# State space stage: one scan instruction of 1024 columns a unit in place of two of 512, its decays in two buffers

## The chip, the cores and the metric

The kernel runs on one core of one Trainium2 chip. The metric is the device time in microseconds (us) from launch to end; less is better. The engines that matter here are TensorE (PE), VectorE (DVE), ScalarE (ACT), GpSimd (POOL) and SyncE (SP), which issues the DMAs of this stage. SBUF and PSUM are the two on-chip memories.

## The reference

A pre-norm layer with a state space block (Mamba) is followed by a pre-norm layer with attention and a mixture of eight experts. The input is 16 sequences of 1024 tokens of 256 features, in fp32. The change is in the state space block only, whose heart is this recurrence over the tokens, for 512 channels d and 16 states n:

```python
def step(h, inp):
    d_t, B_t, C_t, u_t = inp
    dA = jnp.exp(d_t[:, :, None] * A)
    h = h * dA + (d_t * u_t)[:, :, None] * B_t[:, None, :]
    y = jnp.einsum('bdn,bn->bd', h, C_t)
    return (h, y)
```

`d_t` (delta) is a softplus of a projection, `u_t` the convolved input, `y + u * D` is gated by `silu(z)` and projected out. The decay `dA` differs for each channel, state and token.

## The kernel before

The program runs four stages one after the other: the state space stage (lines 79 to 768), attention, routing, experts. Only the first changes.

**Tiling.** Each of the 16 sequences is cut into two halves of T = 512 tokens. The 512 channels are four groups of 128 (the partitions). A half is worked as 32 units: two passes of two channel groups each (PC = 2), and in a pass the 16 states. So a unit is one state `n` of two channel groups `c`, 128 x 2 x 512 elements, and there are 16 x 2 x 32 = 1024 units. For the second half of a sequence the scan starts from `h_end`, which holds the last column of every unit of the first half.

**One unit.** SyncE loads the row B of the state on all partitions (`bb`), and the row C (`cb` or `cv`). GpSimd multiplies `du` by `bb` to `dbu` (line 361, 128x1024). ScalarE makes the decays, one `Exp` of 512 columns for each channel group, into `decay` in PSUM (line 512). VectorE scans each group (line 622, `tensor_tensor_scan`, h = h * decay + dbu). The state is then weighed by C to `prod`: by GpSimd in 13 of 32 units (line 370, u % 5 in 1 and 3), by VectorE in the other 19 (line 604), where ScalarE has first copied the row C into PSUM as `c_bank` (line 499). TensorE sums the products of the 16 states in PSUM by matmuls with the identity (line 739).

**Rings.** `bb`, `dbu`, `h` and `prod` are rings of four units (RING). `decay` has one slot for each of the two groups, all of it two PSUM banks; `c_bank` has one, `y_bank` two, and three `side` banks serve the preparation of the next half (normalisation, input projection, convolution, delta, silu), which all engines do between the steps of the units, at the 64 positions of a hand-written table (SIDE).

**Order.** Every engine has its own program, written out by hand; the engines meet only at semaphores. GpSimd's order for unit u is: make `dbu` of unit u + 2, then weigh unit u - 1 if that is its own. The waits around the scan are:

```python
wait(act, scan_done, scans_done(q, u - 1, cc))   # ScalarE, before decay[:, cc] of unit u
wait(pool, scan_done, scans_done(q, u - RING))   # GpSimd, before dbu of unit u
wait(pool, scan_done, scans_done(q, u))          # GpSimd, before it weighs unit u
```

Of the kernel before, what the change touches and what calls it, by code (L numbers as in the profile page):

```python
# [8 lines left out]
ALU = mybir.AluOpType  # L9
# [3 lines left out]
P = 128  # L13
# [5 lines left out]
T = 512  # L19
# [41 lines left out]
def mamba_stage(nc, x, w, x1, rows_bc):  # L61
# [65 lines left out]
    with ExitStack() as ctx:  # L127
# [31 lines left out]
        sp_r = sb("sp_r", [P, CH, T])  # L159
# [42 lines left out]
        decay_done = sem("decay_done")  # L202
        scan_done = sem("scan_done")
# [33 lines left out]
        def scans_done(q, u, cc=PC - 1):  # L237
            return count(q, POSITIONS, PC * u + cc + 1)
# [91 lines left out]
        def _(pool):  # L330
# [24 lines left out]
            def make_dbu(q, u):  # L355
                p, slot = u // NS, u % RING
                wait(pool, b_loaded[slot], count(q, 16 * (UNITS // RING), 16 * (u // RING + 1)))
                wait(pool, scan_done, scans_done(q, u - RING))
                if u % NS == 0:
                    wait(pool, du_done, count(q, PASSES, p + 1))  # L360
                nc.gpsimd.tensor_tensor(  # L361
                    dbu[:, slot], du[:, q[1], p * PC:(p + 1) * PC], bb[:, slot].unsqueeze(1).to_broadcast([P, PC, T]),
                    ALU.mult).then_inc(dbu_done, 1)

            def weigh_state(q, u):
                k, slot = POOL_UNITS.index(u), u % RING
                wait(pool, c_loaded[C_BUFFER[k]], count(q, 16 * loads_into(C_BUFFER, k), 16 * loads_into(C_BUFFER, k, k + 1)))
                wait(pool, scan_done, scans_done(q, u))
# [32 lines left out]
        def _(act):  # L401
# [7 lines left out]
            act.wait_ge(s_a, 4)  # L409
# [12 lines left out]
            def take(q, kind, i):  # L422
# [26 lines left out]
                elif kind == "dbl":  # L449

                    wait(act, rows_stored, count(before(before(q)), 32, 32))
                    ins = nc.scalar.copy(dbl[:, r], bank)
                elif kind == "dt":
                    if i == 0:
                        wait(act, delta_done, count(q, CH, 0))
                    nc.scalar.activation(sp_r[:, i], bank, ACT.Relu, bias=vecs[:, 1, i:i + 1])
                    ins = nc.scalar.activation(bank, bank, ACT.Abs, bias=vecs[:, 1, i:i + 1])
# [34 lines left out]
            def save_end(q, u):  # L492
                wait(act, scan_done, scans_done(q, u))
                nc.scalar.copy(h_end[:, u], h[:, u % RING, :, T - 1]).then_inc(end_saved, 1)

# [5 lines left out]
            def scan_block(q, last, norm):  # L501
                r = q[1]
                wait(act, delta_done, count(q, CH, CH))
                for u in range(UNITS):
                    n = u % NS
                    for cc in range(PC):
                        c = u // NS * PC + cc
                        to, earlier = unit_at(q, u - 2)
                        if cc and earlier in VECTOR_UNITS:
                            copy_c(q, vector_upto(earlier) % VU)  # L510
                        wait(act, scan_done, scans_done(q, u - 1, cc))
                        nc.scalar.activation(decay[:, cc], delta[:, r, c], ACT.Exp,  # L512
                                             scale=a_neg[:, c, n:n + 1]).then_inc(decay_done, 1)
                        if not last:
                            prepare(after(q), PC * u + cc, norm)
# [12 lines left out]
        def _(dve):  # L528
# [56 lines left out]
            def preparation(q, v, norm):  # L585
# [7 lines left out]
                if dt_of and dt_of[0] == "dt":  # L593
                    c = dt_of[1]
                    wait(dve, soft_done, count(p, 2 * CH, 2 * c + 2))
                    nc.vector.tensor_tensor(delta[:, p[1], c], side_bank[:, bank_of("dt", c)], sp_r[:, c],
                                            ALU.add).then_inc(delta_done, 1)

            def weigh_state(q, u):
                slot = u % RING  # L600
                wait(dve, scan_done, scans_done(q, u))
# [5 lines left out]
            def scan_block(q, last, norm):  # L607
                r = q[1]
                for u in range(UNITS):
                    n, slot = u % NS, u % RING  # L610
                    for cc in range(PC):
                        wait(dve, decay_done, scans_done(q, u, cc))
                        if cc == 0:
                            wait(dve, dbu_done, units_done(q, u))
                            to, earlier = unit_at(q, u - RING)
                            if not (first(q) and u < RING):
                                wait(dve, prod_by_pool, count(to, PU, pool_upto(earlier)))
                            if r:
                                wait(dve, end_saved, q[0] * UNITS + min(UNITS, UNITS - RING + u + 1))
                            else:  # L620
                                wait(dve, end_saved, q[0] * UNITS + (u - RING + 1 if u >= RING else 0))
# [3 lines left out]
                        if cc == 0:  # L625
                            to, earlier = unit_at(q, u - 1)
                            if earlier in VECTOR_UNITS and not (first(q) and u == 0):
                                weigh_state(to, earlier)
# [1207 lines left out]
```

## Time and profile before

| | |
|---|---|
| median of 3 runs | 6550.24 us (6548.16 to 6550.28) |
| the profiled execution's own time | 6549.9 us |
| its span, first to last instruction | 6548.2 us |
| mean granted TensorE clock | 0.976 of full speed |
| state space stage | 0 to about 3613 us of the span |
| busy over the span | PE 94%, DVE 65%, ACT 54%, POOL 78% |

The profile is one execution. Busy shares over the whole span mix four stages; the last (experts, from about 4400 us) is TensorE's and GpSimd's DMAs. So the stretch 400 to 3500 us is read for this change, and other stages only for durations that the state space stage does not show. In a timeline row the first number is the start, the second the length, and xN says how many instructions are merged in it.

### The profile page before, as it was taken

To read this page: it belongs to the slowest core of one execution; us is meant where nothing else is said; L and a number is where in the kernel's file an instruction comes from. 1 tells how busy PE (TensorE), PEld (TensorE's weight loads), DVE (VectorE), ACT (ScalarE), POOL (GpSimd) and SP (SyncE) were. 2 spreads that over 40 slices of the span, in tenths; PEclk is the share of its full clock that TensorE was granted. 3 is DMA by queue.
4 is the path that set the end of the run, shared out by engine and by line. 5 is a ranking of instruction groups with operands and counts; after the bars stand their busy time and mean duration, and the time that the engine had idled before them with its cause. 6 is when DMAs were issued, how large, how long until landed. Compare 5 with 4: busy or idle time off the path is not lost. (4 is left out here: it accounts for less than half of the span.)

```text
span 6548.2 us, 78761 instructions
## 1 busy us (share of the span) xinstructions
PE 6175.3 (94%) x25444; PEld 3970.3 (61%) x25444; DVE 4267.1 (65%) x5490; ACT 3519.6 (54%) x6418; POOL 5132.0 (78%) x3926
## 2 busy tenths in 40 slices
PE   7999999999999999999998799978999999999999
PEld 3444444444444444444443588866788888888888
DVE  6999999999999999999999377779100000000000
ACT  5677677767676777676766588750222222222222
POOL 6999999999999999999999677736454545454544
PEclk9999999999999999999999999989999999999999
DMA  3555555555555555555555244330566656566554
GB/s 124 166 162 171 166 168 166 168 165 168 165 172 163 166 165 166 170 164 169 166 163 167 62 121 122 116 120 1 175 190 179 190 179 189 180 189 179 183 162 135
DMA packets 551754, 1029.76 MB, mean 157 GB/s; under 512 B 77426, under 2 KB 245876, under 8 KB 516784
## 3 DMA queue, kind: packets, MB, share of 16 engines
q1 hardware_dynamic: 441168, 669.34, 33.3%
q0 software_dynamic: 110176, 355.39, 18.0%
q8 instruction: 204, 3.34, 0.2%
q14 instruction: 206, 1.69, 0.1%
HBM read 926.04 MB, written 88.72 MB: 155 GB/s over the span
## 5 line engine op out<-in xcount | busy, mean ns | idle before, releaser
L361 POOL TENSOR_TENSOR m_dbu<-m_du,m_bb 128x1024 f32<-128x1024 f32 x1024 | 2390.8, 2363 | 0.0
L739 PE MATMUL m_y_bank<-m_prod,m_ident 128*128 128x512 f32 x4096 | 1977.8, 612 | 143.1 <-POOL m_prod L370 143.1
L512 ACT ACTIVATE m_decay<-m_delta,m_a_neg 128x512 f32<-128x512 f32 x2048 | 1419.4, 695 | 724.7 <-DVE m_h L622 722.7
L739 PEld LDWEIGHTS m_y_bank<-m_prod,m_ident 128*128 128x128 f32 x4096 | 789.2, 196 | 1122.9 <-issue 907.2
L1734 DVE TENSOR_SCALAR e_ye<-e_ybank,e_listing 128x256 f32<-128x256 f32 x270 | 118.2, 479 | 1817.1 <-PE e_ybank L1768 1817.1
L622 DVE TENSOR_TENSOR_SCAN m_h<-m_decay,m_h_end,m_dbu 128x512 f32<-128x512 f32 x1024 | 1259.4, 1267 | 3.4 <-ACT m_decay L512 2.5
L622 DVE TENSOR_TENSOR_SCAN m_h<-m_decay,m_dbu 128x512 f32<-128x512 f32 x1024 | 1197.7, 1207 | 13.8 <-ACT m_decay L512 13.2
L1708 ACT ACTIVATE e_a<-e_ubank 128x512 f32<-128x512 f32 x540 | 322.5, 597 | 1473.6 <-PE e_ubank L1759 1473.6
L370 POOL TENSOR_TENSOR m_prod<-m_h,m_cb 128x1024 f32<-128x1024 f32 x416 | 982.5, 2362 | 20.0 <-issue 15.0
L1759 PE MATMUL e_ubank<-e_xT,e_w 128*128 128x256 f32 x4320 | 978.6, 380 | 1.3 <-ACT e_xT L1699 1.3
L1768 PE MATMUL e_ybank<-e_w,e_a 128*128 128x256 f32 x4320 | 954.5, 379 | 0.7 <-ACT e_a L1708 0.7
L1768 PEld LDWEIGHTS e_ybank<-e_w,e_a 128*128 128x128 f32 x4320 | 820.7, 190 | 112.6 <-ACT e_a L1708 1.1
L1651 POOL DMA_INDIRECT e_w<-in_w,weight_row x270 | 258.3, 957 | 799.0 <-PE e_ybank L1768 734.4
L1759 PEld LDWEIGHTS e_ubank<-e_xT,e_w 128*128 128x128 f32 x4320 | 811.6, 190 | 106.7 <-issue 1.6
L604 DVE TENSOR_TENSOR m_prod<-m_h,m_c_bank 128x1024 f32<-128x1024 f32 x608 | 727.3, 1196 | 42.5 <-ACT m_c_bank L499 22.4
L1668 POOL DMA_INDIRECT out<-e_ye,e_token x270 | 429.2, 1590 | 111.0 <-issue 81.3
L706 PE MATMUL m_side<-m_xnT,m_w_in 128*128 128x512 f32 x1024 | 503.0, 600 | 6.0 <-ACT m_xnT L428 6.0
L711 PE MATMUL m_side<-m_xpad,m_tap_diag 128*128 128x512 f32 x1024 | 495.7, 592 | 0.0
L499 ACT COPY m_c_bank<-m_cv 128x512 f32<-128x512 f32 x608 | 359.3, 591 | 95.3 <-DVE m_prod L604 93.1
L706 PEld LDWEIGHTS m_side<-m_xnT,m_w_in 128*128 128x128 f32 x1024 | 198.9, 195 | 260.3 <-issue 258.1
L1659 POOL DMA_INDIRECT e_xe<-n,e_token x270 | 283.8, 1051 | 85.4 <-issue 82.0
L711 PEld LDWEIGHTS m_side<-m_xpad,m_tap_diag 128*128 128x128 f32 x1024 | 194.3, 190 | 245.3 <-issue 245.3
(216 smaller groups left out, 6663.9 us busy)
## 6 DMA issues: line engine op xcount, KB each, us to landing
m_bb<-rows_bc SPq DMA_DIRECT2D x1024, 256.0 KB, 3.8
m_cv<-rows_bc SPq DMA_DIRECT2D x608, 256.0 KB, 4.0
m_cb<-rows_bc SPq DMA_DIRECT2D x416, 256.0 KB, 3.4
m_xin<-in_x SPq DMA_DIRECT2D x32, 512.0 KB, 5.7
m_xres<-in_x SPq DMA_DIRECT2D x32, 512.0 KB, 5.6
x<-m_xres SPq DMA_DIRECT2D x32, 512.0 KB, 6.3
a_xa<-x SPq DMA_DIRECT2D x64, 256.0 KB, 2.9
a_xr<-x SPq DMA_DIRECT2D x64, 256.0 KB, 3.2
```

The costliest lines, as they stand in the source:

```text
L361: nc.gpsimd.tensor_tensor(dbu[:, slot], du[:, q[1], p * PC:(p + 1) * PC], bb[:, slot].unsqueeze(1).to_broadcast([P, PC, T]), ALU.mult).the ...
L370: nc.gpsimd.tensor_tensor(prod[:, slot], h[:, slot], cb[:, C_BUFFER[k]].unsqueeze(1).to_broadcast([P, PC, T]), ALU.mult).then_inc(prod_by_ ...
L499: nc.scalar.copy(c_bank[:], cv[:, V_BUFFER[k]]).then_inc(c_copied, 1)
L512: nc.scalar.activation(decay[:, cc], delta[:, r, c], ACT.Exp, scale=a_neg[:, c, n:n + 1]).then_inc(decay_done, 1)
L604: nc.vector.tensor_tensor(prod[:, slot], h[:, slot], c_bank[:].unsqueeze(1).to_broadcast([P, PC, T]), ALU.mult).then_inc(prod_by_vector, 1)
L622: nc.vector.tensor_tensor_scan(h[:, slot, cc], decay[:, cc], dbu[:, slot, cc], h_end[:, u, cc:cc + 1] if r else 0.0, ALU.mult, ALU.add).th ...
L706: ins = nc.tensor.matmul(bank, w_in[:, piece, col:col + P], xnT[:, piece], start=(piece == 0), stop=final)
L711: ins = nc.tensor.matmul(bank, tap_diag[:, i, piece], xpad[:, i, piece:piece + T], start=(piece == 0), stop=final)
L739: ins = nc.tensor.matmul(y_bank[:, cc], ident[:], prod[:, slot, cc], start=False, stop=(n == NS - 1))
L1668: nc.gpsimd.indirect_dma_start(out, bass.IndirectOffsetOnAxis(ap=token[:, col:col + 1], axis=0), ye[:, n % Y_RING, j], None, compute_op=AL ...
L1759: ins = nc.tensor.matmul(ubank[:, (n * UG + g) % U_RING, i], w1[:, r, k, c * P:(c + 1) * P], xT[:, n % 2, k], start=(k == 0), stop=(k == K ...
L1768: ins = nc.tensor.matmul(ybank[:, n % 2, j], a[:, n % 2, c, j * P:(j + 1) * P], w2[:, n % W_RING, c], start=(c == 0), stop=(c == FC - 1))
```

## The change

Both groups of a unit are scanned by one instruction over 1024 columns. A scan carries its state from each column to the next, so at column 512 (the first of the second group) the state of the first group would run on. To cut it there the decay of that column is made 0 once, at the start of the stage, in each of two buffers, and the `Exp` of the second group writes columns 1 to 511 only. In the first half of a sequence the scan then starts from 0 by itself. In the second half the second group must start from `h_end`: ScalarE adds `h_end * first_decay` to the first column of `dbu` of that group (`carry`, one column, once a unit), where `first_decay` is made by two small `Exp` at the head of the half, and VectorE waits for it (`carried`).

The decays now have two buffers, so that ScalarE writes those of unit u while unit u - 1 is scanned: units with even u keep the two PSUM banks (`decay_even`, shown as m_decay), units with odd u use `decay_odd` in SBUF. `sp_r`, a scratch of the preparation, shrinks from four slots to two to make room, and its waits follow. SBUF tensors and PSUM tensors are told apart by `sb` and `al.ps` in the code.

```diff
-        sp_r = sb("sp_r", [P, CH, T])
+        sp_r = sb("sp_r", [P, 2, T])
+        first_decay = sb("first_decay", [P, PASSES, NS])
+        decay_odd = sb("decay_odd", [P, PC, T])
-        decay = al.ps("decay", [P, PC, T])
+        decay_even = al.ps("decay", [P, PC, T])
...
+        def decay_of(u):
+            return decay_odd if u % 2 else decay_even
...
+            for of in (decay_even, decay_odd):
+                nc.scalar.mul(of[:, 1, 0:1], ident[:, 0:1], 0.0).then_inc(s_a, 1)
...
+            def carry(q, u):
+
+                start = dbu[:, u % RING, 1, 0:1]
+                wait(act, first_done, PASSES * (q[0] + 1))
+                wait(act, end_saved, carries(q[0], u))
+                wait(act, dbu_done, units_done(q, u))
+                nc.scalar.activation(start, h_end[:, u, 1:2], ACT.Identity, scale=first_decay[:, u // NS, u % NS:u % NS + 1],
+                                     bias=start).then_inc(carried, 1)
...
+                if r:
+                    wait(act, carried, carries(q[0] - 1, UNITS - 1))
+                    for p in range(PASSES):
+                        c = p * PC + 1
+                        nc.scalar.activation(first_decay[:, p], a_neg[:, c], ACT.Exp,
+                                             scale=delta[:, r, c, 0:1]).then_inc(first_done, 1)
...
-                        wait(act, scan_done, scans_done(q, u - 1, cc))
-                        nc.scalar.activation(decay[:, cc], delta[:, r, c], ACT.Exp,
+                        wait(act, scan_done, units_done(q, u - 2))
+                        nc.scalar.activation(decay_of(u)[:, cc, cc:], delta[:, r, c, cc:], ACT.Exp,
                                              scale=a_neg[:, c, n:n + 1]).then_inc(decay_done, 1)
+                        if cc and r:
+                            carry(q, u)
...
-                    for cc in range(PC):
-                        wait(dve, decay_done, scans_done(q, u, cc))
...
-                        nc.vector.tensor_tensor_scan(h[:, slot, cc], decay[:, cc], dbu[:, slot, cc],
-                                                     h_end[:, u, cc:cc + 1] if r else 0.0,
-                                                     ALU.mult, ALU.add).then_inc(scan_done, 1)
+                    wait(dve, decay_done, decays_done(q, u))
+                    if r:
+                        wait(dve, carried, carries(q[0], u))
...
+                    nc.vector.tensor_tensor_scan(
+                        h[:, slot].rearrange("p c t -> p (c t)"), decay_of(u)[:].rearrange("p c t -> p (c t)"),
+                        dbu[:, slot].rearrange("p c t -> p (c t)"), h_end[:, u, 0:1] if r else 0.0,
+                        ALU.mult, ALU.add).then_inc(scan_done, 1)
```

The order of instructions on TensorE, GpSimd and SyncE is the same as before. On VectorE it changes as follows, shown for the first units of the second half of the first sequence. Before, with each scan 512 columns long (the listing names a scan by its instruction format, SCALAR_TENSOR_TENSOR) and `m_prod` the product of VectorE's own units:

```order
L622 SCALAR_TENSOR_TENSOR m_h<-m_decay,m_h_end,m_dbu 128x512 x3
L604 TENSOR_TENSOR m_prod<-m_h,m_c_bank 128x1024
L622 SCALAR_TENSOR_TENSOR m_h<-m_decay,m_h_end,m_dbu 128x512 x2
L566 TENSOR_TENSOR m_zs<-m_y_bank,m_zs 128x512
L622 SCALAR_TENSOR_TENSOR m_h<-m_decay,m_h_end,m_dbu 128x512
L566 TENSOR_TENSOR m_zs<-m_y_bank,m_zs 128x512
L622 SCALAR_TENSOR_TENSOR m_h<-m_decay,m_h_end,m_dbu 128x512
L604 TENSOR_TENSOR m_prod<-m_h,m_c_bank 128x1024
```

The same place now; the scan of every second unit reads `m_decay_odd`:

```order
L651 SCALAR_TENSOR_TENSOR m_h<-m_decay,m_h_end,m_dbu 128x1024
L651 SCALAR_TENSOR_TENSOR m_h<-m_decay_odd,m_h_end,m_dbu 128x1024
L633 TENSOR_TENSOR m_prod<-m_h,m_c_bank 128x1024
L651 SCALAR_TENSOR_TENSOR m_h<-m_decay,m_h_end,m_dbu 128x1024
L595 TENSOR_TENSOR m_zs<-m_y_bank,m_zs 128x512 x2
L651 SCALAR_TENSOR_TENSOR m_h<-m_decay_odd,m_h_end,m_dbu 128x1024
L633 TENSOR_TENSOR m_prod<-m_h,m_c_bank 128x1024
```

Each pair of scans has become one, and what stood between the two scans of a unit (a product, a gate) now stands behind the one.

On ScalarE, at the head of the same half, the rows are now these (`m_first_decay` and the one-column write to `m_dbu` are new; before, there were only the decays, the copies to `m_c_bank` and `m_h_end` and the preparation):

```order
L529 ACTIVATE m_first_decay<-m_a_neg,m_delta 128x16 x2
L539 ACTIVATE m_decay<-m_delta,m_a_neg 128x512
L520 COPY m_c_bank<-m_cv 128x512
L539 ACTIVATE m_decay<-m_delta,m_a_neg 128x511
L514 ACTIVATE m_dbu<-m_h_end,m_dbu,m_first_decay 128x1
L506 COPY m_h_end<-m_h 128x2
L539 ACTIVATE m_decay_odd<-m_delta,m_a_neg 128x512
L539 ACTIVATE m_decay_odd<-m_delta,m_a_neg 128x511
L514 ACTIVATE m_dbu<-m_h_end,m_dbu,m_first_decay 128x1
```

The number of decays is the same; one small instruction a unit is added in second halves, and odd units' decays go to SBUF.

## Rows read from the trace of the kernel before

**Rows 1.** The page: span, and busy time of each engine (share, instructions).

```profile
span 6548.2 us, 78761 instructions
...
PE 6175.3 (94%) x25444; PEld 3970.3 (61%) x25444; DVE 4267.1 (65%) x5490; ACT 3519.6 (54%) x6418; POOL 5132.0 (78%) x3926
```

**Rows 2.** Busy time of each engine in a stretch, TensorE clock, DMA share, GB/s.

```profile
core 0: us, PE busy (x) PEld busy (x) DVE busy (x) ACT busy (x) POOL busy (x), PEclk, DMA share, GB/s
400.00:3500.00 3100.00, 2944.55 (x7159) 1341.94 (x7160) 3011.55 (x3039) 2191.09 (x3938) 3082.69 (x1424) 0.98 0.54 167
```

**Rows 3.** The same for the stretch that holds the end of the stage.

```profile
3500.00:3700.00 200.00, 136.57 (x442) 78.19 (x440) 124.34 (x148) 92.18 (x158) 152.64 (x181) 0.90 0.38 114
```

**Rows 4.** GpSimd by line, 0 to 3613 us: busy us, mean ns, idle before.

```profile
L361 POOL TENSOR_TENSOR m_dbu<-m_du,m_bb 128x1024 f32<-128x1024 f32 x1024 | 2390.8, 2363 | 0.0
L370 POOL TENSOR_TENSOR m_prod<-m_h,m_cb 128x1024 f32<-128x1024 f32 x416 | 982.5, 2362 | 20.0 <-issue 15.0 <-DVE m_h L622 5.0
L353 POOL TENSOR_TENSOR m_du<-m_delta,m_xc 128x1024 f32<-128x1024 f32 x64 | 151.0, 2360 | 11.0 <-DVE m_delta L596 11.0
L345 POOL TENSOR_TENSOR m_rstd<-m_rstd,m_minus_half 128x4 f32<-128x4 f32 x32 | 32.3, 1008 | 2.5
L347 POOL TENSOR_TENSOR m_shift<-m_shift,m_rstd 128x4 f32<-128x4 f32 x32 | 6.4, 201 | 2.5
L343 POOL TENSOR_TENSOR m_shift<-m_moments,m_minus_one 128x4 f32<-128x4 f32 x32 | 6.4, 201 | 0.0
L342 POOL TENSOR_TENSOR m_rstd<-m_moments,m_eps 128x4 f32<-128x4 f32 x32 | 6.3, 198 | 47.2 <-DVE m_moments L545 47.2
```

**Rows 5.** Timeline of GpSimd: start us, length us, instructions merged (xcount); first work.

```profile
59.55 2.35 POOL L353 TENSOR_TENSOR m_du<-m_delta,m_xc 128x1024 f32<-128x1024 f32 x1 [6.73 <-DVE m_delta L596]
...
68.30 11.61 POOL L361 TENSOR_TENSOR m_dbu<-m_du,m_bb 128x1024 f32<-128x1024 f32 x5
```

**Rows 6.** Timeline of GpSimd, the end of the stage.

```profile
3612.31 2.34 POOL L370 TENSOR_TENSOR m_prod<-m_h,m_cb 128x1024 f32<-128x1024 f32 x1 [4.13 <-DVE m_h L622]
```

**Rows 7.** VectorE by line, 0 to 3613 us.

```profile
L622 DVE TENSOR_TENSOR_SCAN m_h<-m_decay,m_h_end,m_dbu 128x512 f32<-128x512 f32 x1024 | 1259.4, 1267 | 3.4 <-ACT m_decay L512 2.5
L622 DVE TENSOR_TENSOR_SCAN m_h<-m_decay,m_dbu 128x512 f32<-128x512 f32 x1024 | 1197.7, 1207 | 13.8 <-ACT m_decay L512 13.2
L604 DVE TENSOR_TENSOR m_prod<-m_h,m_c_bank 128x1024 f32<-128x1024 f32 x608 | 727.3, 1196 | 42.5 <-ACT m_c_bank L499 22.4 <-issue 19.5 <-DVE m_h L622 0.6
```

**Rows 8.** Timeline of VectorE inside a sequence.

```profile
2004.14 3.63 DVE L622 TENSOR_TENSOR_SCAN m_h<-m_decay,m_h_end,m_dbu 128x512 f32<-128x512 f32 x3
```

**Rows 9.** One line each: duration ns min/median/max.

```profile
L361 POOL TENSOR_TENSOR m_dbu<-m_du,m_bb x1024: 2332/2358/2449, 68.3 to 3603.5; 128x1024 f32<-128x1024 f32 x171
```

**Rows 10.** The same for the scans, and who waited for them.

```profile
L622 DVE TENSOR_TENSOR_SCAN m_h<-m_decay,m_dbu x1024: 1187/1210/1225, 72.1 to 3507.8; 128x512 f32<-128x512 f32 x171
L622 DVE TENSOR_TENSOR_SCAN m_h<-m_decay,m_h_end,m_dbu x1024: 1245/1271/1285, 181.9 to 3610.9; 128x512 f32<-128x512 f32 x171
...
  ACT m_decay L512: 722.7, 1221
```

**Rows 11.** Waits, 400 to 3500 us: who for whom, us in total, times, longest.

```profile
ACT m_decay L512 <- DVE m_h L622: 622.0, 1047, 2.5
```

**Rows 12.** Timeline in the attention stage, GpSimd and VectorE at once.

```profile
3801.43 0.19 POOL L1005 TENSOR_TENSOR a_tmp<-a_moments,a_eps 128x2 f32<-128x2 f32 x1
3801.48 1.34 DVE L1217 TENSOR_SCALAR a_n<-a_hid,a_moments,a_rs 128x256 f32<-128x256 f32 x2
...
3801.59 0.18 POOL L1006 TENSOR_TENSOR a_minus_mean<-a_moments,a_minus_one 128x2 f32<-128x2 f32 x1
3801.85 1.33 POOL L1007 TENSOR_TENSOR a_rs<-a_tmp,a_minus_half 128x2 f32<-128x2 f32 x1
```

**Rows 13.** Timeline of VectorE late in that stage, GpSimd idle.

```profile
4359.72 0.74 DVE L1217 TENSOR_SCALAR a_n<-a_hid,a_moments,a_rs 128x256 f32<-128x256 f32 x2 [1.08 <-POOL a_rs L1022]
```

**Rows 14.** GpSimd power on two columns beside such VectorE work: min/median/max.

```profile
L1007 POOL TENSOR_TENSOR a_rs<-a_tmp,a_minus_half x64: 692/962/1426, 3640.2 to 4233.5; 128x2 f32<-128x2 f32 x64
```

**Rows 15.** The same operation a little later in each item.

```profile
L1013 POOL TENSOR_TENSOR a_rr<-a_tmp,a_minus_half x64: 692/693/697, 3642.1 to 4235.8; 128x2 f32<-128x2 f32 x64
```

**Rows 16.** VectorE, normalisation in the attention stage: min/median/max.

```profile
L1217 DVE TENSOR_SCALAR a_n<-a_hid,a_moments,a_rs x128: 315/754/1339, 3801.5 to 4379.5; 128x256 f32<-128x256 f32 x128
```

**Rows 17.** Routing stage, VectorE with both inputs in SBUF: mean ns.

```profile
L1545 DVE TENSOR_TENSOR_SCAN r_rank<-r_ones,r_total 128x128 f32<-128x128 f32 x8 | 2.6, 399 | 3.7 <-PE r_total L1477 3.7
L1532 DVE TENSOR_TENSOR r_best<-r_line,r_desc 128x1024 f32<-128x1024 f32 x2 | 2.5, 1226 | 0.1
```

**Rows 18.** ScalarE by line, 0 to 3613 us: the decays and the small copy.

```profile
L512 ACT ACTIVATE m_decay<-m_delta,m_a_neg 128x512 f32<-128x512 f32 x2048 | 1419.4, 695 | 724.7 <-DVE m_h L622 722.7
...
L494 ACT COPY m_h_end<-m_h 128x2 f32<-128x2 f32 x512 | 95.0, 185 | 0.0
```

More of the change, by code:

```diff
@@ L202, in mamba_stage @@
         decay_done = sem("decay_done")
+        first_done = sem("first_done")
+        carried = sem("carried")
         scan_done = sem("scan_done")
@@ L235, in units_done, with decays_done, carries @@
             return count(q, UNITS, u + 1)
-        def scans_done(q, u, cc=PC - 1):
-            return count(q, POSITIONS, PC * u + cc + 1)
+        def decays_done(q, u):
+            return count(q, POSITIONS, PC * (u + 1))
+        def decay_of(u):
+            return decay_odd if u % 2 else decay_even
+        def carries(b, u):
+            return b * UNITS + u + 1
         @block.sync
@@ L357, in make_dbu @@
                 wait(pool, b_loaded[slot], count(q, 16 * (UNITS // RING), 16 * (u // RING + 1)))
-                wait(pool, scan_done, scans_done(q, u - RING))
+                wait(pool, scan_done, units_done(q, u - RING))
                 if u % NS == 0:
@@ L367, in weigh_state @@
                 wait(pool, c_loaded[C_BUFFER[k]], count(q, 16 * loads_into(C_BUFFER, k), 16 * loads_into(C_BUFFER, k, k + 1)))
-                wait(pool, scan_done, scans_done(q, u))
+                wait(pool, scan_done, units_done(q, u))
                 wait(pool, summed, units_done(q, u - RING))
@@ L453, in take @@
                 elif kind == "dt":
-                    if i == 0:
-                        wait(act, delta_done, count(q, CH, 0))
-                    nc.scalar.activation(sp_r[:, i], bank, ACT.Relu, bias=vecs[:, 1, i:i + 1])
+                    wait(act, delta_done, count(q, CH, i - 1))
+                    nc.scalar.activation(sp_r[:, i % 2], bank, ACT.Relu, bias=vecs[:, 1, i:i + 1])
                     ins = nc.scalar.activation(bank, bank, ACT.Abs, bias=vecs[:, 1, i:i + 1])
@@ L600, in weigh_state @@
                 slot = u % RING
-                wait(dve, scan_done, scans_done(q, u))
+                wait(dve, scan_done, units_done(q, u))
                 wait(dve, c_copied, count(q, VU, vector_upto(u)))
@@ new lines, in scan_block @@
+                    slot = u % RING
+                    wait(dve, decay_done, decays_done(q, u))
+                    if r:
+                        wait(dve, carried, carries(q[0], u))
+                    wait(dve, dbu_done, units_done(q, u))
+                    to, earlier = unit_at(q, u - RING)
+                    if not (first(q) and u < RING):
+                        wait(dve, prod_by_pool, count(to, PU, pool_upto(earlier)))
+                    if r:
+                        wait(dve, end_saved, q[0] * UNITS + min(UNITS, UNITS - RING + u + 1))
+                    else:
+                        wait(dve, end_saved, q[0] * UNITS + (u - RING + 1 if u >= RING else 0))
@@ new lines, in scan_block @@
+                    nc.vector.tensor_tensor_scan(
+                        h[:, slot].rearrange("p c t -> p (c t)"), decay_of(u)[:].rearrange("p c t -> p (c t)"),
+                        dbu[:, slot].rearrange("p c t -> p (c t)"), h_end[:, u, 0:1] if r else 0.0,
+                        ALU.mult, ALU.add).then_inc(scan_done, 1)
+                    to, earlier = unit_at(q, u - 1)
+                    if earlier in VECTOR_UNITS and not (first(q) and u == 0):
+                        weigh_state(to, earlier)
```

20 lines of the change are left out of this document (3 added, 17 removed).

## The prediction, made before the changed kernel ran

> **What bounds the kernel now.** The busy shares of the page [rows 1] mix four stages, so the first view to read is the busy time of the stretch 400 to 3500 us [rows 2]: of 3100 us GpSimd is busy 3082.69 (99.4%), VectorE 3011.55 (97.1%), TensorE 2944.55 (95%), ScalarE 2191.09 (71%). Two engines are close to full, so the second view is GpSimd by line [rows 4]: 1024 products `dbu`, 416 `prod` and 64 `du`, all of 128x1024, and small operations of 32.3 + 6.4 + 6.4 + 6.3 = 51.4 us. Five of them back to back take 11.61 us [rows 5], so one follows the other after (11.61 - 2.35) / 4 = 2.315 us. The sum of the work is 1504 x 2.315 + 51 = 3533 us. It begins at 59.55 us [rows 5] and ends at 3612.31 + 2.34 = 3614.65 us [rows 6], that is 3555 us. So the stage is GpSimd's queue from end to end, with 22 us of idle time. Behind it comes the wait view: ScalarE waits 622.0 us for scans [rows 11], because `decay` has one slot a group. That wait looks large, and it is on an engine with 29% to spare.
>
> VectorE is next. A unit takes 3555 / 1024 = 3.47 us, of which it works 97%, 3.37 us: two scans (1207 ns, or 1267 with `h_end` [rows 7]), which follow one another after (3.63 - 1.27) / 2 = 1.18 us [rows 8], and the product and preparation.
>
> **What the change removes.** One start of a scan a unit. No scan of 1024 columns is in this trace. From 128 columns at 399 ns [rows 17] to 512 at 1207 [rows 7] a column costs 808 / 384 = 2.10 ns, so 1024 take 399 + 896 x 2.10 = 2284 ns without and 2344 with `h_end` (the 60 ns between 1267 and 1207), mean 2.31 us. From that the overlap with the next instruction goes off, 1.27 - 1.18 = 0.09 us: 2.22 us against 2 x 1.18 = 2.36. VectorE gains 0.14 us a unit, 143 us in all. None of it reaches the end, since GpSimd's 3533 us of work stay. The second buffer lets ScalarE work a unit ahead and ends much of its 622 us of waits; that is worth nothing to GpSimd either. What the two together could give is part of the 22 us of idle time.
>
> **What it adds on ScalarE.** 512 carries of one column, at the 185 ns of the copy of two columns [rows 18]: 95 us, and two small `Exp` in each of 16 halves, 32 x 0.2 = 6 us. Together 0.1 us a unit on an engine that works 2.46 of 3.47 us. The carry stands in front of the scan and behind `dbu` of its own unit. Queued behind it on ScalarE are the next preparation step and the decays of the unit after, for which the scan waits; GpSimd runs up to three units ahead of the scan, so what the chain gains or loses here is at most a VectorE wait, cost 0. If the cover were gone, it would be about 0.3 us in each of 512 units, 150 us. Decays written to SBUF in odd units are not shown either; a decay now takes 695 ns [rows 18] and even half as much again in every second unit would leave ScalarE idle. `sp_r` with two slots makes ScalarE wait for a VectorE addition that is two units old: nothing.
>
> **What it adds on GpSimd, the term that decides.** Until now no large VectorE instruction of this stage read two tensors in SBUF: the scans read `decay` and the products `c_bank`, both in PSUM. GpSimd's products last 2332/2358/2449 ns at least, in the middle and at most [rows 9] and the scans 1187/1210/1225 [rows 10], so beside each other they are undisturbed. In odd units the scan now reads `decay_odd` and `dbu`, both in SBUF. Does that disturb GpSimd? The state space stage cannot say, but the attention stage has one case of VectorE work from SBUF to SBUF beside GpSimd. The normalisation (a pair) takes 0.74 us when GpSimd is idle [rows 13] and 1.34 beside it [rows 12]. The power on GpSimd that meets it takes 1.33 us there, and 692/693/697 ns where nothing meets it [rows 15]; over the 64 items it ranges 692/962/1426 [rows 14], as the normalisation does, 315/754/1339 [rows 16]. Both grow by about what the other lasts: 0.60 us against 0.69, and 0.64 against 0.74. From 3801.43 to 3801.85 + 1.33 = 3803.18 both together take 1.75 us; one after the other they would be 0.74 + 0.19 + 0.18 + 0.69 = 1.80. They take turns, they do not share. A two-input operation on 1024 columns in SBUF takes 1226 ns in the routing stage, where GpSimd is not at work [rows 17], so the form in itself is not slow.
>
> The Trainium skill (SBUF — State Buffer, "Who interferes with whom") states the same for this very form: a VectorE instruction with two SBUF inputs takes the read interface that GpSimd reads through, and who comes second is blocked for the whole of the other's instruction. The rows above agree for another form, a normalisation of one tensor; for a scan no row here shows it. By that rule the whole duration of an odd scan goes onto GpSimd's queue; by the rows of this stage alone, where nothing disturbs anything, the sum would be 0.
>
> I take the turns. Then GpSimd stands still while each of the 512 odd scans runs: 512 x 2.31 = 1185 us. Handing over costs something between 0 (the 1.75 us above are less than 1.80) and 0.1 us (the longest power, 1426 - 693 = 733 ns, is about the pair of 740): 0.05 x 512 = 26 us. VectorE in its turn waits for the GpSimd product that is running, up to 2.315 us per pair of units. It has the room: its work per pair is 2 x (3.37 - 0.14) = 6.46 us, with that wait 8.8, and GpSimd's cycle is (3533 + 1185 + 26) / 512 = 9.27. TensorE falls from 95% to 95 x 3.47 / 4.63 = 71% busy. In a stretch with 68% its granted clock is 0.90, near the full 2.4 GHz [rows 3]; a fall to 1.2 GHz I hold for unlikely.
>
> **Sum.** 6549.9 (the profiled execution, 0.3 us under the median) + 1185 + 26 = 7761, so 7760 us.
>
> **The range of this case.** If the starting part of a scan does not hold the interface, each costs 399 - 128 x 2.10 = 130 ns less, 67 us in all, and without handing over 26 less: 7670. With 0.1 us for each handing over and 0.2 us of mismatch between the two engines per pair of units it is 7760 + 26 + 102 = 7890.
>
> **The rivals.**
>
> *GpSimd keeps its turn.* Its instructions follow each other without a gap, so VectorE may get in only where GpSimd stops at a semaphore. After an odd scan u it has `dbu` of u + 4 to make, 2.315 us, and then needs scan u + 1, which VectorE ends after about 2.22 + 1.1 = 3.3 us; 1.0 us of idle time, unless it weighs unit u itself (7 of 16 odd units). 9/16 x 1.0 x 512 = 290 us more: 8050. For it speaks the closed queue, against it that the power in [rows 12] grew although it stood in such a queue.
>
> *They share by the word.* A scan of 1024 columns takes 1024 reads of the interface; GpSimd makes 2048 in 2.315 us, 1.13 ns each. The odd scan then costs 1.16 us: 512 x 1.16 = 592 us, 7140 in all. Against it speak the 1.75 against 1.80 us.
>
> *No contention: not slower.* If only the normalisation's kind of instruction takes the second interface and a scan does not, GpSimd's 3533 us of work stay and with them the time: 6550, at best 22 us less, 6528. The point from which it decides is the median of line 361: at 2358 ns there is nothing to pay. For it speaks that no row shows a two-input VectorE instruction beside GpSimd.
>
> **How the numbers follow.** Turns: 0.62. GpSimd keeps its turn: 0.09. By the word: 0.13. No contention: 0.16, of which 0.07 gains over 0.2% (13 us, about what a measurement of this kernel can tell from no change) and 0.09 does not. The predicted time is that of the turns, 7760. A range that leaves out the last case and takes in the others, with 50 us below 7140 and 10 above 8050, is 7090 to 8060; the likeliest case's own is 7670 to 7890. Faster 0.07, same 0.09, slower 0.84.
>
> **What would show it.** In the stretch 400 to 3500 us the products of line 361 should have two lengths, about 2.36 and up to 4.7 us, with a mean near 2.36 + 1185 / 1504 = 3.15 us; scans from `m_decay` near 2.28 us always, scans from `m_decay_odd` between 2.3 and 4.6. GpSimd stays at 99% busy, since blocked time counts as busy. Units come every 4.6 us. ScalarE's waits for scans grow, since everything is slower. The prediction is wrong if scans from both buffers have one duration and line 361 stays at 2358 ns; it is wrong in size if only one of the two engines stretches, or if VectorE waits for `carried` or TensorE's clock falls to half and takes the bound.

## The result, and the profile after

The changed kernel takes 7744.2 us (median of 4 runs, 7738.5 to 7750.34) against 6550.24: ratio 1.1824, 95% interval 1.1803 to 1.1844. That is 16 us under the predicted 7760. The time came out as forecast, but the profile shows that it is made up otherwise: the predicted mechanism is there and smaller than forecast, and a second one, which was not predicted, stands beside it. The page of the kernel after:

```profile
span 7739.2 us, 78889 instructions
...
PE 6562.2 (85%) x25444; PEld 4044.8 (52%) x25444; DVE 4804.5 (62%) x4466; ACT 3611.4 (47%) x6964; POOL 5733.3 (74%) x3926
```

Busy time of each engine from 400 to 4700 us, columns as in [rows 2]:

```profile
400.00:4700.00 4300.00, 3399.48 (x7401) 1453.12 (x7400) 3616.10 (x2228) 2357.99 (x4584) 3748.07 (x1478) 0.91 0.40 125
```

GpSimd is busy 3748.07 of 4300 us, 87%, where it was 99.4% in [rows 2]. VectorE is at 84% (it was 97%). TensorE is 79% busy, at a mean granted clock of 0.91; with only the two levels of 2.4 and 1.2 GHz that is some 18% of the stretch at the lower one (0.98 before: 4%). No engine is full any more: somewhere they wait for one another. GpSimd by line over the stage (busy us, mean ns, idle before and whom it waited for), which answers to [rows 4]:

```profile
L372 POOL TENSOR_TENSOR m_dbu<-m_du,m_bb 128x1024 f32<-128x1024 f32 x1024 | 2930.6, 2879 | 254.6 <-DVE m_h L651 253.0 <-issue 0.2
L381 POOL TENSOR_TENSOR m_prod<-m_h,m_cb 128x1024 f32<-128x1024 f32 x416 | 1008.9, 2425 | 263.4 <-DVE m_h L651 248.6 <-issue 14.8
L364 POOL TENSOR_TENSOR m_du<-m_delta,m_xc 128x1024 f32<-128x1024 f32 x64 | 172.2, 2690 | 101.7 <-DVE m_delta L625 101.7
```

A `dbu` product takes 2879 ns instead of 2363. That is (2879 - 2363) x 1024 = 528 us, and with `prod` (63 ns x 416 = 26) and `du` (330 ns x 64 = 21) GpSimd's products have grown by 575 us. It is also idle in front of them for 254.6 + 263.4 + 101.7 = 620 us; before, it was 31. Together 575 + 589 = 1164 us of the 1191 by which the span grew. The scans, min/median/max in ns, in answer to [rows 10]:

```profile
L651 DVE TENSOR_TENSOR_SCAN m_h<-m_decay,m_dbu x256: 2255/2290/2292, 73.4 to 4648.6; 128x1024 f32<-128x1024 f32 x128
L651 DVE TENSOR_TENSOR_SCAN m_h<-m_decay_odd,m_dbu x256: 2290/3662/4503, 75.6 to 4653.3; 128x1024 f32<-128x1024 f32 x128
L651 DVE TENSOR_TENSOR_SCAN m_h<-m_decay,m_h_end,m_dbu x256: 2317/2349/2351, 217.7 to 4794.5; 128x1024 f32<-128x1024 f32 x128
L651 DVE TENSOR_TENSOR_SCAN m_h<-m_decay_odd,m_h_end,m_dbu x256: 2323/3522/4540, 219.9 to 4799.6; 128x1024 f32<-128x1024 f32 x128
```

Scans whose decays are in PSUM last 2290 and 2349 ns in the middle, all within 40 ns; the prediction had 2284 and 2344. Scans that read `decay_odd` in SBUF last between 2290 and 4540. What VectorE waited for before its scans (us in total, times, longest):

```profile
DVE m_h L651 <- ACT m_decay L539: 410.4, 320, 2.0
DVE m_h L651 <- ACT m_decay_odd L539: 328.3, 325, 2.5
...
DVE m_h L651 <- ACT m_dbu L514: 14.7, 15, 1.9
```

Together 753 us; before, 17 [rows 7]. So VectorE, too, has two kinds of loss: odd scans are longer, and it waits for decays. Both can be seen in one stretch of 9 us. VectorE (start, length, operation, idle before):

```profile
2009.71 1.19 DVE L633 TENSOR_TENSOR m_prod<-m_h,m_c_bank 128x1024 f32<-128x1024 f32 x1
2012.60 2.35 DVE L651 TENSOR_TENSOR_SCAN m_h<-m_decay,m_h_end,m_dbu 128x1024 f32<-128x1024 f32 x1 [1.70 <-ACT m_decay L539]
2015.14 3.57 DVE L651 TENSOR_TENSOR_SCAN m_h<-m_decay_odd,m_h_end,m_dbu 128x1024 f32<-128x1024 f32 x1 [0.19 <-ACT m_dbu L514]
```

GpSimd in the same stretch:

```profile
2014.21 2.35 POOL L381 TENSOR_TENSOR m_prod<-m_h,m_cb 128x1024 f32<-128x1024 f32 x1
2016.51 4.35 POOL L372 TENSOR_TENSOR m_dbu<-m_du,m_bb 128x1024 f32<-128x1024 f32 x1
```

**Taking turns.** The odd scan is issued at 2015.14, while GpSimd's `prod` runs until 2016.56. It ends at 2018.71, 2.15 us behind that. GpSimd's next product, issued at 2016.51, takes 4.35 us instead of 2.35: it stood still for 2.00 us, and ends at 2020.86, 2.15 us behind the scan. The scan waited for the product that ran, and the next product waited for the scan. Alone each lasts 2.35 us, so each did about 0.2 us of its work beside the other. The experiments call this cost the turns.

**The other wait.** VectorE's product ends at 2009.71 + 1.19 = 2010.90 and its even scan starts at 2012.60, 1.70 us later, behind a decay. ScalarE in between:

```profile
2010.99 0.59 ACT L520 COPY m_c_bank<-m_cv 128x512 f32<-128x512 f32 x1 [3.49 <-DVE m_prod L633]
2011.51 0.69 ACT L539 ACTIVATE m_decay<-m_delta,m_a_neg 128x511 f32<-128x511 f32 x1
2012.14 0.37 ACT L514 ACTIVATE m_dbu<-m_h_end,m_dbu,m_first_decay 128x1 f32<-128x1 f32 x1
```

ScalarE copies the row C into `c_bank` (line 520) as soon as the product of VectorE has read it (idle 3.49 us before), then makes the second decay (511 columns), then the carry, and only then the scan can start. The copy for the next of VectorE's units stands between the two decays in ScalarE's queue, as it did before the change. Before, what stood behind it was only the decay of the second group, and VectorE had the scans of two groups (the second of the unit before, the first of this one) to do meanwhile. Now the one scan of the unit needs both decays. So a chain (product, copy, decay, carry, scan) lies open after each of VectorE's products that no other work of VectorE covers. The experiments call this cost the chain. ScalarE's rows for the copy, before and after, over the whole stage, show where its idle time went:

```profile
L499 ACT COPY m_c_bank<-m_cv 128x512 f32<-128x512 f32 x608 | 359.3, 591 | 95.3 <-DVE m_prod L604 93.1
```

```profile
L520 ACT COPY m_c_bank<-m_cv 128x512 f32<-128x512 f32 x608 | 358.6, 590 | 1744.2 <-DVE m_prod L633 1744.2
```

Before, ScalarE waited 93 us in front of its copies for VectorE's products; now it waits 1744 us there, with the second decay queued behind.

### The profile page after: what moved, and what is told of

It reads as the page before. It is cut to its first block and busy times, and to the rows that moved or that the text cites. A ratio compares the mean times of both kernels' runs of the same rounds, so it can differ in the third digit from the quotient of the medians.

```text
span 7739.2 us, 78889 instructions
## 1 busy us (share of the span) xinstructions
PE 6562.2 (85%) x25444; PEld 4044.8 (52%) x25444; DVE 4804.5 (62%) x4466; ACT 3611.4 (47%) x6964; POOL 5733.3 (74%) x3926
## 5 line engine op out<-in xcount | busy, mean ns | idle before, releaser
L372 POOL TENSOR_TENSOR m_dbu<-m_du,m_bb 128x1024 f32<-128x1024 f32 x1024 | 2930.6, 2879 | 254.6 <-DVE m_h L651 253.0
L769 PE MATMUL m_y_bank<-m_prod,m_ident 128*128 128x512 f32 x4096 | 2177.4, 663 | 516.6 <-DVE m_prod L633 321.9
L769 PEld LDWEIGHTS m_y_bank<-m_prod,m_ident 128*128 128x128 f32 x4096 | 832.6, 211 | 1672.9 <-issue 926.8
L381 POOL TENSOR_TENSOR m_prod<-m_h,m_cb 128x1024 f32<-128x1024 f32 x416 | 1008.9, 2425 | 263.4 <-DVE m_h L651 248.6
L651 DVE TENSOR_TENSOR_SCAN m_h<-m_decay_odd,m_dbu 128x1024 f32<-128x1024 f32 x256 | 888.6, 3471 | 161.4 <-ACT m_decay_odd L539 159.4
L651 DVE TENSOR_TENSOR_SCAN m_h<-m_decay_odd,m_h_end,m_dbu 128x1024 f32<-128x1024 f32 x256 | 870.9, 3402 | 183.9 <-ACT m_decay_odd L539 168.9
L539 ACT ACTIVATE m_decay_odd<-m_delta,m_a_neg 128x512 f32<-128x512 f32 (+1 forms) x1024 | 719.6, 715 | 128.5 <-DVE m_h L651 128.5
L651 DVE TENSOR_TENSOR_SCAN m_h<-m_decay,m_h_end,m_dbu 128x1024 f32<-128x1024 f32 x256 | 599.3, 2341 | 234.6 <-ACT m_decay L539 234.6
L633 DVE TENSOR_TENSOR m_prod<-m_h,m_c_bank 128x1024 f32<-128x1024 f32 x608 | 723.9, 1191 | 0.0
L539 ACT ACTIVATE m_decay<-m_delta,m_a_neg 128x512 f32<-128x512 f32 (+1 forms) x1024 | 688.4, 682 | 41.9 <-DVE m_h L651 41.9
L651 DVE TENSOR_TENSOR_SCAN m_h<-m_decay,m_dbu 128x1024 f32<-128x1024 f32 x256 | 584.1, 2282 | 175.7 <-ACT m_decay L539 175.7
L736 PE MATMUL m_side<-m_xnT,m_w_in 128*128 128x512 f32 x1024 | 549.5, 635 | 118.7 <-DVE m_delta L625 51.9
```

The costliest lines, as they stand in the source:

```text
L372: nc.gpsimd.tensor_tensor(dbu[:, slot], du[:, q[1], p * PC:(p + 1) * PC], bb[:, slot].unsqueeze(1).to_broadcast([P, PC, T]), ALU.mult).the ...
L381: nc.gpsimd.tensor_tensor(prod[:, slot], h[:, slot], cb[:, C_BUFFER[k]].unsqueeze(1).to_broadcast([P, PC, T]), ALU.mult).then_inc(prod_by_ ...
L539: nc.scalar.activation(decay_of(u)[:, cc, cc:], delta[:, r, c, cc:], ACT.Exp, scale=a_neg[:, c, n:n + 1]).then_inc(decay_done, 1)
L633: nc.vector.tensor_tensor(prod[:, slot], h[:, slot], c_bank[:].unsqueeze(1).to_broadcast([P, PC, T]), ALU.mult).then_inc(prod_by_vector, 1)
L651: nc.vector.tensor_tensor_scan(h[:, slot].rearrange("p c t -> p (c t)"), decay_of(u)[:].rearrange("p c t -> p (c t)"), dbu[:, slot].rearra ...
L736: ins = nc.tensor.matmul(bank, w_in[:, piece, col:col + P], xnT[:, piece], start=(piece == 0), stop=final)
```

## The experiments

Seven kernels ran. The first three and the changed kernel make a table of two by two: with and without a second input in SBUF (the turns), with and without the copy in front of the second decay (the chain). Differences to the kernel before are taken from the runs of it made beside each experiment (6550.6 us for the first four, 6550.03 for the last three).

### The copy behind the decays

```diff
-                        if cc and earlier in VECTOR_UNITS:
-                            copy_c(q, vector_upto(earlier) % VU)
                         wait(act, scan_done, units_done(q, u - 2))
...
                         if cc and r:
                             carry(q, u)
+                        if cc and earlier in VECTOR_UNITS:
+                            copy_c(q, vector_upto(earlier) % VU)
```

> The changed kernel with one move: ScalarE copies the row C into c_bank after both decays (and the carry) of a unit, not between them. The work is the same. Theory of two costs (VectorE and GpSimd take turns at the odd scans, and the chain product, copy, second decay, scan leaves VectorE idle): the chain is gone, GpSimd becomes the bound with 3533 us of work and 512 x 2.0 us of standing still (2.0 us is what a blocked product is longer in the trace, 4.35 against 2.35), so 6550 + 1024 = about 7570. Turns alone: the copy has no part in it, 7740 stays. Chain alone: back to about 6550. If GpSimd only loses what its products now show (577 us), about 7130.

Measured: 7547.71 us, ratio 1.1524 (1.1504 to 1.1543), 196 us less than the changed kernel. The busy times from 500 to 2500 us, and GpSimd by line:

```profile
500.00:2500.00 2000.00, 1618.56 (x3591) 709.88 (x3592) 1774.92 (x1084) 1148.53 (x2220) 1997.80 (x718) 0.91 0.40 130
```

```profile
L372 POOL TENSOR_TENSOR m_dbu<-m_du,m_bb 128x1024 f32<-128x1024 f32 x1024 | 2925.0, 2879 | 0.0
L381 POOL TENSOR_TENSOR m_prod<-m_h,m_cb 128x1024 f32<-128x1024 f32 x416 | 1303.4, 3133 | 2.3 <-issue 2.3
L364 POOL TENSOR_TENSOR m_du<-m_delta,m_xc 128x1024 f32<-128x1024 f32 x64 | 273.9, 4280 | 10.8 <-DVE m_delta L625 10.8
L353 POOL TENSOR_TENSOR m_rstd<-m_moments,m_eps 128x4 f32<-128x4 f32 x32 | 36.0, 1125 | 47.4 <-DVE m_moments L574 47.4
```

GpSimd is busy 1997.80 of 2000 us and is the bound. Its growth is (2879 - 2363) x 1024 + (3133 - 2362) x 416 + (4280 - 2360) x 64 + 30 (line 353) = 528 + 321 + 123 + 30 = 1002 us, and the kernel is 997 us slower than before. This is the case that the prediction described, and here it can be priced cleanly: 997 / 512 = 1.95 us for each odd scan, so 7548 where 7570 was expected. That the copy has no part in it is refuted by the 196 us, that the chain is all of it by the 997.

### Odd scans read PSUM

```diff
-                nc.scalar.copy(c_bank[:], cv[:, V_BUFFER[k]]).then_inc(c_copied, 1)
+                nc.scalar.mul(c_bank[:], cv[:, V_BUFFER[k]], 0.1).then_inc(c_copied, 1)
...
+                    source = c_bank[:, 0:1].to_broadcast([P, PC * T]) if u % 2 else decay_even[:].rearrange("p c t -> p (c t)")
...
-                        h[:, slot].rearrange("p c t -> p (c t)"), decay_of(u)[:].rearrange("p c t -> p (c t)"),
+                        h[:, slot].rearrange("p c t -> p (c t)"), source,
```

> The changed kernel, where the scan of an odd unit takes as decay the first column of c_bank in PSUM (0.1 C, the same for all 1024 columns) in place of decay_odd in SBUF; ScalarE still makes decay_odd, nobody reads it, and the copy of C is scaled by 0.1. So the computation is another one, the instructions and waits are the same. It takes away the second SBUF input alone. Two costs: no turns, all products of GpSimd near 2.36 us and odd scans near 2.3, but the chain stays: VectorE works 3.31 us a unit and idles 0.72, 4.03 x 1024 = 4127 us against 3555, so about 7120. Turns alone (the prediction): 6550. Chain alone: 7740.

Measured: 7209.84 us, ratio 1.1010 (1.0992 to 1.1029). `dbu` on GpSimd, min/median/max, and the four kinds of scan (busy, mean, idle before, releaser):

```profile
L372 POOL TENSOR_TENSOR m_dbu<-m_du,m_bb x1024: 2332/2354/2408, 68.2 to 4255.1; 128x1024 f32<-128x1024 f32 x171
```

```profile
L656 DVE TENSOR_TENSOR_SCAN m_h<-m_c_bank,m_h_end,m_dbu 128x1024 f32<-128x1024 f32 x256 | 600.1, 2344 | 218.2 <-ACT m_decay_odd L543 185.3 <-ACT m_dbu L518 33.0
L656 DVE TENSOR_TENSOR_SCAN m_h<-m_decay,m_h_end,m_dbu 128x1024 f32<-128x1024 f32 x256 | 599.9, 2344 | 238.9 <-ACT m_decay L543 235.8 <-issue 3.1
L656 DVE TENSOR_TENSOR_SCAN m_h<-m_decay,m_dbu 128x1024 f32<-128x1024 f32 x256 | 584.7, 2284 | 177.8 <-ACT m_decay L543 176.8
L656 DVE TENSOR_TENSOR_SCAN m_h<-m_c_bank,m_dbu 128x1024 f32<-128x1024 f32 x256 | 584.3, 2282 | 161.4 <-ACT m_decay_odd L543 161.4
```

With no second input in SBUF, GpSimd's products are back at 2354 ns in the middle and 2408 at most, and all scans at 2282 or 2344. The kernel stays 659 us slower than before, and the idle time in front of the scans is 218.2 + 238.9 + 177.8 + 161.4 = 796 us, nearly all behind decays. The expected 7120 was 90 us too low. The idle time is 796 us, not the 739 that the two decay waits of the changed kernel came to, which is 57 us of it; the other 33 were not traced.

### Neither

Odd scans read `c_bank` as in the run before; beyond that:

```diff
-                        if later in VECTOR_UNITS and not (ends and to is not q):
-                            load_c_for_vector(to, VECTOR_UNITS.index(later))
...
-                        if cc and earlier in VECTOR_UNITS:
-                            copy_c(q, vector_upto(earlier) % VU)
...
-                wait(dve, c_copied, count(q, VU, vector_upto(u)))
```

> As the run before, and ScalarE never copies C (c_bank holds zeros from the start, VectorE's products and the odd scans use it; its 608 loads of the row C are left out too). Both suspected costs are gone. All three theories say that GpSimd's 3533 us of work bound the stage again: 6530 to 6550. More than 6600 would mean a third cost, in the fused scan, the carry or the second buffer itself.

Measured: 6571.99 us, ratio 1.0034 (1.0021 to 1.0046). From 500 to 2500 us, and GpSimd's two large lines:

```profile
500.00:2500.00 2000.00, 1879.90 (x4587) 854.79 (x4585) 1880.74 (x1379) 1282.33 (x2484) 1976.12 (x915) 0.98 0.38 121
```

```profile
L369 POOL TENSOR_TENSOR m_dbu<-m_du,m_bb 128x1024 f32<-128x1024 f32 x1024 | 2398.2, 2378 | 0.0
L378 POOL TENSOR_TENSOR m_prod<-m_h,m_cb 128x1024 f32<-128x1024 f32 x416 | 987.5, 2374 | 20.5 <-DVE m_h L650 20.3 <-issue 0.2
```

The fused scan, the two buffers and 512 carries together cost almost nothing once the two causes are away, and they gain nothing either: VectorE falls to 94% busy and GpSimd stays at 99%. The small `sp_r` with its waits and the decays of odd units written to SBUF are in this kernel too, so neither of them costs anything by itself. The 21 us that are left go with products of 2378 and 2374 ns on GpSimd, 15 and 12 ns longer than in [rows 4], 20 us over 1440 products. Why they are longer here, when they were 2356 in the run before, was not tried and stays open.

### The old scans with odd decays in SBUF

```diff
+        decay_odd = sb("decay_odd", [P, PC, T])
...
-                        nc.scalar.activation(decay[:, cc], delta[:, r, c], ACT.Exp,
+                        nc.scalar.activation((decay_odd if u % 2 else decay)[:, cc], delta[:, r, c], ACT.Exp,
...
-                        nc.vector.tensor_tensor_scan(h[:, slot, cc], decay[:, cc], dbu[:, slot, cc],
+                        nc.vector.tensor_tensor_scan(h[:, slot, cc], (decay_odd if u % 2 else decay)[:, cc], dbu[:, slot, cc],
```

> The kernel before, with two scans of 512 columns a unit and all its waits, where only the decays of odd units lie in SBUF (sp_r with two slots makes the room, with its waits). One part of the change alone. Turns: each of the two odd scans waits for the GpSimd product that runs and then blocks the next one; per pair of units VectorE needs 6.7 us + 2 x up to 2.3 = up to 11.3, GpSimd 6.9 + 2 x 1.1 = 9.1; between 7650 and 8800, nearer the upper end. Chain alone: the old order has no such chain, so 6550.

Measured: 7601.0 us, ratio 1.1604 (1.1585 to 1.1623). From 500 to 2500 us, `dbu` on GpSimd, and the scans of first halves:

```profile
500.00:2500.00 2000.00, 1603.39 (x3568) 691.27 (x3567) 1999.52 (x1519) 1109.31 (x1965) 1848.71 (x710) 0.92 0.40 128
```

```profile
L362 POOL TENSOR_TENSOR m_dbu<-m_du,m_bb x1024: 2333/3266/3360, 68.3 to 4649.1; 128x1024 f32<-128x1024 f32 x171
```

```profile
L622 DVE TENSOR_TENSOR_SCAN m_h<-m_decay,m_dbu x512: 1189/1205/1215, 72.1 to 4519.5; 128x512 f32<-128x512 f32 x171
L622 DVE TENSOR_TENSOR_SCAN m_h<-m_decay_odd,m_dbu x512: 1192/2205/3404, 74.4 to 4525.6; 128x512 f32<-128x512 f32 x171
```

The place of half the decays alone, without a fused scan, costs 1050 us. The order of the instructions is the old one; `sp_r` has two slots, with the waits of the changed kernel. Here VectorE is full (1999.52 of 2000), since it can meet a running product twice in an odd unit: its odd scans last 1192 to 3404 ns. The expected range began at 7650 and leaned to its upper end; that was wrong, because a scan does not always meet a product at its start. It waits about 1.0 us in the middle (2205 against 1205), not 2.3. A GpSimd product that meets such a scan of 512 columns takes 3266 ns in the middle against 2358 [rows 9], 0.91 us more. For 1024 columns it was 2.00 us more in the product shown above. The difference is 1.09 us for 512 columns, 2.13 ns a column, which is the scan's own pace (2.10 by the prediction). So what is held grows with the columns, and in both cases it is some 0.2 us less than the columns' own time (1.09 and 2.18 us): the start of the instruction, worth 130 ns in the prediction, does not show in what GpSimd stands still.

### Both buffers in SBUF

The copy stands behind the decays, as in the first experiment; beyond that:

```diff
-        decay_even = al.ps("decay", [P, PC, T])
+        decay_even = sb("decay", [P, PC, T])
```

> The kernel with the copy of C behind the decays (it took 7548 us), and both decay buffers in SBUF. The suspected cost is doubled, nothing else. Turns: every scan blocks GpSimd, whose products grew by 977 us in all for 512 such scans; with 1024 of them 2 x 977, so 6550 + 1954 = about 8500, and GpSimd stays the bound. If the cost were ScalarE writing to SBUF or the wider distance between the engines, far less than that.

Measured: 8561.16 us, ratio 1.3070 (1.3048 to 1.3092), 2011 us slower than before, twice the 997 us of one buffer. GpSimd, and the two kinds of scan of first halves:

```profile
L372 POOL TENSOR_TENSOR m_dbu<-m_du,m_bb 128x1024 f32<-128x1024 f32 x1024 | 3474.2, 3415 | 0.0
L381 POOL TENSOR_TENSOR m_prod<-m_h,m_cb 128x1024 f32<-128x1024 f32 x416 | 1736.4, 4174 | 2.3 <-DVE m_h L651 2.3
```

```profile
L651 DVE TENSOR_TENSOR_SCAN m_h<-m_decay_odd,m_dbu 128x1024 f32<-128x1024 f32 x256 | 999.4, 3904 | 183.7 <-POOL m_dbu L372 69.6 <-ACT m_decay_odd L537 68.7 <-issue 45.3
...
L651 DVE TENSOR_TENSOR_SCAN m_h<-m_decay,m_dbu 128x1024 f32<-128x1024 f32 x256 | 924.6, 3612 | 132.7 <-issue 46.5 <-ACT m_decay_odd L537 43.6 <-POOL m_dbu L372 35.7
```

The scans that read `m_decay`, undisturbed at 2282 ns as long as it was in PSUM, now last 3612 in the mean. Each scan with two inputs in SBUF costs GpSimd its share: 2011 / 1024 = 1.96 us, against 1.95 with 512 such scans.

### One buffer in PSUM

The copy stands behind the decays here too, and `decay_odd` is gone:

```diff
-            return decay_odd if u % 2 else decay_even
+            return decay_even
...
-                        wait(act, scan_done, units_done(q, u - 2))
+                        wait(act, scan_done, units_done(q, u - 1))
```

> The fused scan with its carry and the copy behind the decays, but one decay buffer in PSUM for all units, so that both decays of a unit wait for the whole scan of the unit before. No scan reads two SBUF tensors. By turns and chain: GpSimd's products are back at 2.36 us and a new chain takes their place, scan 2.31, two decays 1.35, in second halves the carry 0.35, some 3.9 to 4.1 us a unit: about 7050 to 7250, faster than with decay_odd in SBUF. If the fused scan itself were the trouble, it would be as slow as the changed kernel, 7744.

Measured: 7311.87 us, ratio 1.1164 (1.1145 to 1.1183), 62 us above the expected range. The scans of both kinds, with the idle time before them:

```profile
L649 DVE TENSOR_TENSOR_SCAN m_h<-m_decay,m_h_end,m_dbu 128x1024 f32<-128x1024 f32 x512 | 1202.8, 2349 | 509.9 <-ACT m_decay L535 326.7 <-ACT m_dbu L512 180.8
L649 DVE TENSOR_TENSOR_SCAN m_h<-m_decay,m_dbu 128x1024 f32<-128x1024 f32 x512 | 1171.6, 2288 | 368.8 <-ACT m_decay L535 364.1
```

The scans are undisturbed (2349 and 2288 ns), and VectorE idles 509.9 + 368.8 = 879 us before them. This is what the second buffer was for: without it the two decays and the carry lie open behind every scan. Even so this is 236 us faster than two buffers of which one is in SBUF, with the same copy behind the decays (7548 us). The expectation had counted 0.35 us for the carry and no preparation step of ScalarE in the chain; the trace has such steps between the two decays of a unit (at 2019.31 us two of 0.67 and 0.65 us). How the 62 us divide was not measured.

### Two GpSimd units given to VectorE

Again on top of the copy behind the decays:

```diff
-    POOL_UNITS = [u for u in range(UNITS) if u % 5 in (1, 3)]
+    POOL_UNITS = [u for u in range(UNITS) if u % 5 in (1, 3) and u not in (8, 23)]
```

> The kernel with the copy of C behind the decays, where VectorE weighs the units 8 and 23 of each half that GpSimd weighed: 64 products of 2.315 us less on GpSimd, 64 of 1.11 us more on VectorE. If GpSimd is the bound of that kernel, as the turns say, it gains 148 us: about 7400. If VectorE is, it loses 71: about 7620.

Measured: 7402.44 us, ratio 1.1301 (1.1282 to 1.1320), 145 us less than with 13 units. From 500 to 2500 us:

```profile
500.00:2500.00 2000.00, 1653.04 (x3736) 723.48 (x3734) 1842.58 (x1151) 1198.05 (x2323) 1997.81 (x711) 0.92 0.42 134
```

The gain is GpSimd's 148 us within 3 us, which shows that GpSimd is the bound when the chain is gone. It is still at 1997.81 of 2000. No version of those tried beats the kernel before.

## Why the prediction was right, and where it was not

**The four corners.** Changed kernel 7744; turns only 7548; chain only 7210; neither 6572. Alone, the turns cost 7548 - 6572 = 976 us and the chain 7210 - 6572 = 638. Together they cost 1172 and not 1614. The two overlap by 442 us: an odd scan that runs while GpSimd waits at a semaphore for VectorE disturbs nobody, and the chain gives GpSimd 620 us of such waiting. GpSimd's rows bear this out: its instructions grew by 1002 us with the turns only and by 575 in the changed kernel, 427 us less. (The two corners without the chain are not made alike: one moves ScalarE's copies, the other leaves them out together with their loads. Odd scans from PSUM with the copy only moved were not run, so how exact the split is stays open.)

**What held.** That the fused scan saves VectorE time which does not reach the end: a scan of 1024 columns takes 2290 and 2349 ns against the 2284 and 2344 worked out, and without the two costs the kernel is not faster than before. That no scan from PSUM disturbs GpSimd. That a scan with both inputs in SBUF takes turns with GpSimd's products: shown by the run that moves only the decays (1.1604), the one that takes the SBUF input away (2354 ns), and the one that doubles it (2011 against 997 us). The Trainium skill (SBUF — State Buffer, "Who interferes with whom") says that a VectorE instruction with two SBUF inputs contends with a GpSimd instruction that reads SBUF, and that the port pair they share is an exclusive lock; that the other is blocked for the whole instruction it says in its line on VectorE's two-port modes, and the prediction took it for scans too. The trace agrees on who blocks whom and on the order, and puts the blocked time at 2.00 us of an undisturbed 2.35.

**What was mis-sized.** The term "GpSimd stands still while each of the 512 odd scans runs: 512 x 2.31 = 1185 us", with 26 us for handing over. It measured 997 us in all where GpSimd is the bound (1.95 us a scan). The prediction had the 130 ns of a scan's start as the lower bound of its range, and should have gone below that. The case that it described is 7548 us, below its own range of 7670 to 7890.

**The step that failed.** On ScalarE, "what the chain gains or loses here is at most a VectorE wait, cost 0". It looked at the carry and at `dbu`, and did not ask what else in ScalarE's queue a fused scan now waits for. The second decay is queued behind the copy of C, the copy behind VectorE's product, and that put 753 us of waits in front of VectorE's scans (17 before); alone it costs 638 us, on top of the turns 196. The prediction did price a lost cover, at 150 us, but by the carry alone. Its sentence that the second buffer ends much of ScalarE's waits for scans held for the decays (722.7 us before [rows 10], 128.5 + 41.9 = 170 after), against its own sign that these waits grow; the idle time moved in front of the copy. The carry was also priced too low, and decays into SBUF are a little longer. ScalarE's rows after, busy us, mean ns:

```profile
L539 ACT ACTIVATE m_decay_odd<-m_delta,m_a_neg 128x512 f32<-128x512 f32 x465 | 332.9, 716 | 109.9 <-DVE m_h L651 109.9
...
L539 ACT ACTIVATE m_decay<-m_delta,m_a_neg 128x512 f32<-128x512 f32 x466 | 317.9, 682 | 35.7 <-DVE m_h L651 35.7
...
L514 ACT ACTIVATE m_dbu<-m_h_end,m_dbu,m_first_decay 128x1 f32<-128x1 f32 x458 | 170.6, 373 | 0.0
```

The carry of one column takes 373 ns, not the 185 of the copy in [rows 18], and a decay to SBUF 716 against 682 ns to PSUM. Neither costs time by itself: the kernel without turns and chain has both, at 6572 us. Inside the chain the carry is one more link in second halves. What decides is the place of the copy. The oversized term (1211 against 997, 214 us too much) and the missing one (196) made up for one another, and that is why 7760 came so near 7744. That nearness is luck. GpSimd "stays at 99% busy" was named as a sign and came out as 87%, and a mean `dbu` near 3.15 us as 2.88: these two signs told that the time had another make-up. The lengths came as named: products of line 372 up to 4.44 us, scans from `m_decay` near 2.3 us, those from `m_decay_odd` up to 4.54.

**The rivals.** "GpSimd keeps its turn" (8050) fell: scans enter behind the running product, 2015.14 against 2016.56 above. "They share by the word" (7140) fell by 2.00 us of standing still where 1.16 was its price, and by scans that themselves wait. "No contention" (6550) fell with GpSimd's products of 4.35 us.

## What to carry to other kernels

When instructions are fused, list everything that the first of them now waits for that only the second waited for before, and look for what stands ahead of it in the other engine's in-order queue; a copy that was hidden between two scans was in front of one. Before a tensor moves from PSUM to SBUF, count the inputs in SBUF of each VectorE instruction that reads it: the second one makes it take turns with GpSimd, and where GpSimd is the bound every such microsecond is paid. A total that agrees proves little; compare the busy share and the mean duration that the forecast implies.

## What the runs showed of the hardware

A `tensor_tensor_scan` in fp32 goes at 2.1 ns a column (399 ns for 128 columns, 1210 for 512, 2290 for 1024), and a start operand read from SBUF adds 60 ns once. With decays and `dbu` both in SBUF it holds up a GpSimd product of two SBUF inputs by 0.91 us for 512 and 2.00 us for 1024 columns, some 0.2 us less than its columns take in either case. A one-column ScalarE operation with scale and bias read from SBUF takes 373 ns, twice a two-column copy. TensorE's mean granted clock in this stage was 0.98 with TensorE busy 95%, 0.91 at 79% to 81%, and 0.83 at 72% (the run with both buffers in SBUF): the lower level of 1.2 GHz was granted for some 4%, 18% and 34% of the time. The prediction called a mean of 0.90 near 2.4 GHz; by the same working it is a mixture with a fifth of the time at 1.2 GHz. With the copy behind the decays this cost nothing that the end saw: the clock was 0.91 there too, and GpSimd was 99.9% busy.
